# Layer 0's mixture of experts: rank products over all 128 rows, exponentials ahead of the codes' copy, sums and experts' products one whole tile later

## What is computed

```
q = einsum('btd,ed->bte', hidden_states, W_q)            # 4 heads, two halves x and y
sim = einsum('pbthn,hkpn->pbthk', q, keys)
scores_xy, idx_xy = top_k(sim, 8)
all_scores = sx[..., :, None] + sy[..., None, :]         # 64 pairs per head
scores, pk = top_k(all_scores, 8)
w = silu(einsum('btd,bthkd->bthk', hidden_states, down_embed[indices]) * softmax(scores))
experts_states = einsum('bthk,bthkd->btd', w, up_embed[indices])
dense = silu(hidden_states @ W_up.T) @ W_down.T
return dense + experts_states
```

## Time and profile before

| | us |
|---|---|
| median of 3 runs (1495.67 to 1496.87) | 1496.2 |
| the profiled execution's own time | 1500.19 |
| its span, first to last instruction | 1498.9 |
| feed-forward loop, first code to last expert product (208.39 to 509.86) | 301.5 |
| PE / DVE / ACT / POOL busy over the span | 1258.3 / 967.3 / 623.6 / 423.1 |

### The profile page before, as it was taken

The page is one execution under the profiler, slowest core; times in us unless marked ns, Lnnn a source line. Parts: engine busy times, 40 slices in busy tenths (PEclk is TensorE's granted clock), DMA queues, the critical chain, the costliest instruction groups (busy, mean ns, idle before and its releaser), DMA issues.

```text
span 1498.9 us, 23059 instructions
## 1 busy us (share of the span) xinstructions
PE 1258.3 (84%) x8094; PEld 828.3 (55%) x8094; DVE 967.3 (65%) x2897; ACT 623.6 (42%) x1625; POOL 423.1 (28%) x691
## 2 busy tenths in 40 slices
PE   5377669888988579999999999999999998577885
PEld 3266625555555446656666665566566665265555
DVE  3588777888876347766666566566666665365465
ACT  1000024444444235555555555555555554412331
POOL 1013241333313124343343333333433433101010
PEclk9598989999999769999999999999999999778797
DMA  6200020000000000000000000000000000000000
GB/s 181 78 1 1 1 85 1 1 1 1 1 1 1 0 0 1 1 2 1 1 1 2 1 1 1 1 1 1 1 1 1 1 1 1 0 3 5 8 8 8
DMA packets 18402, 15.33 MB, mean 10 GB/s; under 512 B 2416, under 2 KB 16752, under 8 KB 18160
## 3 DMA queue, kind: packets, MB, share of 16 engines
q1 hardware_dynamic: 18288, 13.86, 3.1%
HBM read 12.81 MB, written 1.05 MB: 9 GB/s over the span
## 4 chain that ended last, share of the span: by engine, by line
PE 62%; DVE 19%; ACT 9%; issue 7%; POOL 1%; SPq 0%; DMA 0%; DVEq 0%; ACTq 0%; POOLq 0%
PE bank L1395 11%; PE bank L1439 10%; PE bank L1405 8%; PE bank L1596 4%; ACT prb L1464 4%; PE bank L917 3%; PE bank L1349 3%; PE bank L1727 2%; PE bank L1380 2%; DVE negmax L1544 2%; DVE moe L1788 2%; PE bank L1372 2%; PE bank L1399 2%; PE bank L1359 2%; PE bank L902 2%
## 5 line engine op out<-in xcount | busy, mean ns | idle before, releaser
L1490 POOL TENSOR_SCALAR prb<-prb,rnorm 128x512 f32<-128x512 f32 (+3 forms) x512 | 272.5, 549 | 477.9 <-DVE rnorm L1561 475.7
L1464 ACT ACTIVATE prb<-bank,negmax 128x512 f32<-128x512 f32 (+3 forms) x512 | 264.4, 525 | 288.1 <-DVE negmax L1544 283.9
L1544 DVE TENSOR_REDUCE negmax<-bank 128x1 f32<-128x512 f32 (+3 forms) x512 | 219.2, 480 | 126.6 <-PE bank L1399 124.9
L1395 PE MATMUL bank<-kT,qT 64*128 64x512 f32 (+3 forms) x1024 | 202.2, 479 | 3.2 <-ACT prb L1464 3.2
L1405 PE MATMUL bank<-ident,prb 128*128 128x128 f32 x1280 | 193.0, 282 | 3.0 <-POOL prb L1490 1.9
L1405 PEld LDWEIGHTS bank<-ident,prb 128*128 128x128 f32 x1280 | 141.4, 142 | 49.5 <-issue 24.9
L1439 PE MATMUL bank<-prbT,vv 128*64 128x512 f32 (+3 forms) x1024 | 151.9, 439 | 1.7 <-issue 0.8
L1552 DVE COPY prbT<-bank 128x512 f32<-128x512 f32 x128 | 87.7, 685 | 87.0 <-PE bank L1405 87.0
L1395 PEld LDWEIGHTS bank<-kT,qT 64*128 64x128 f32 x1024 | 77.8, 186 | 52.7 <-issue 37.5
L1464 ACT ACTIVATION_READ_ACCUMULATOR prb<-bank,negmax 128x1 f32 x512 | 102.2, 200 | 0.0
L1439 PEld LDWEIGHTS bank<-prbT,vv 128*64 128x64 f32 x1024 | 63.8, 136 | 67.7 <-issue 60.4
(11 more groups left out here) (438 smaller groups left out, 2126.8 us busy)
## 6 DMA issues: line engine op xcount, KB each, us to landing
ew2T<-in_ew2T SPq DMA_DIRECT2D x1, 1024.0 KB, 6.4
ew<-in_ew SPq DMA_DIRECT2D x1, 1024.0 KB, 5.7
wq<-in_Wq SPq DMA_DIRECT2D x2, 512.0 KB, 4.9
wk<-in_Wk SPq DMA_DIRECT2D x2, 512.0 KB, 7.0
wv<-in_Wv SPq DMA_DIRECT2D x1, 1024.0 KB, 7.9
out<-res SPq DMA_DIRECT2D x16, 64.0 KB, 1.5
wmod<-in_wmod SPq DMA_DIRECT2D x2, 384.0 KB, 3.9
c_filt_sb<-in_c_filt SPq DMA_DIRECT2D x1, 768.0 KB, 7.0
```

The costliest lines, as they stand in the source:

```text
L1395: T.matmul(s_of(j, s, i, qc), q[r, qc * P:(qc + 1) * P], k[r, 0:(qc + 1) * P], start=True, stop=False)
L1464: A.activation(prb[j % 2][:, i, p_at[qc]:p_at[qc] + (qc + 1) * P], s_of(j, s, i, qc), ACT.Exp, bias=negmax[j % 2][:, place[qc], i:i + 1], ...
L1490: last = G.tensor_scalar(v, v, rnorm[j % 2][:, place[qc], i:i + 1], 1.0, ALU.mult, ALU.mult)
L1544: V.tensor_reduce(negmax[j % 2][:, place[qc], i:i + 1], s_of(j, s, i, qc), AX.X, ALU.max, negate=True).then_inc(at_max, 1)
```

## The change

1. `sel_y` and `sel_x` get rows of zeros, so that both rank products run over all 128 rows of `codeT`. The outputs are the same; the constants grow and `iota_y` and its neighbours move by 224 words.
2. ACT: `exp(n,0)` and `exp(n,1)` stand ahead of `keep_code(n)`, `keep_past_gate(n)` behind all four `exp`. `keep_sums` and PE's `sums`, `dense`, `experts` and DVE's `result` are done for tile n-2 in step n, one of each in every step.
3. PE: `logit(n,2)` stands between `code(n)` and the ranks, `logit(n,3)` behind ranks 0 and 1, `sums(n-2)` between these and ranks 2 and 3, and `dense(n-2)` and `experts(n-2)` behind them. Both `logit(n+1,.)` stand ahead of `down(n+1)`. Of the two `up` of an odd step the first stands ahead of them, the second behind `down(n+1)`, and from the second batch on both use bank 6.
4. ACT: at the end of an odd step all four `silu` of the two tiles stand in a row.

```diff
--- before.py
+++ after.py
@@ -244,13 +244,13 @@
         prob = [at.take(f"prob{i}", [P, PH, EXPERTS]) for i in range(3)]
         wT = at.take("wT", [P, EXPERTS // P, P])
         codeT = [at.take(f"codeT{i}", [P, 3 * P], BF16) for i in range(2)]
-        assert at.at <= 15264
-        at = Region(15264)
+        assert at.at <= 15040
+        at = Region(15040)
         iota_y = at.take("iota_y", [P, KEYS, TOP], BF16)
         iota_x = at.take("iota_x", [P, XROWS, TOP], BF16)
         rank_ident = at.take("rank_ident", [P, TOP, P], BF16)
-        sel_y = at.take("sel_y", [P, XROWS * KEYS], BF16)
-        sel_x = at.take("sel_x", [P, PH, EXPERTS], BF16)[0:PH * XROWS, :, :]
+        sel_y = at.take("sel_y", [P, 2, EXPERTS], BF16)
+        sel_x = at.take("sel_x", [P, PH, EXPERTS], BF16)
         assert at.at <= 2 * LANE
         at = Region(RAW + 6144)
         gT = [at.take(f"gT{i}", [P, I_UP // P, S]) for i in range(2)]
@@ -444,9 +444,8 @@
             for l in range(2):
                 A.activation(silT[:, l, :], cT[l][:, :], ACT.Silu).then_inc(silu_c, 1)
             for i in range(2):
-                r = slice(KEYS * i, KEYS * i + KEYS)
-                A.activation(sel_y[r, :].rearrange("q (i j) -> q i j", j=KEYS), ident[r, r].unsqueeze(1).broadcast_to([KEYS, XROWS, KEYS]),
-                             ACT.Copy).then_inc(const_ready, 1)
+                A.activation(sel_y[:, i, :].rearrange("q (i j) -> q i j", j=KEYS),
+                             ident[:, KEYS * i:KEYS * i + KEYS].unsqueeze(1).broadcast_to([P, XROWS, KEYS]), ACT.Copy).then_inc(const_ready, 1)
             A.wait_ge(lam_sum, 1)
             A.activation(lam_s[:, :], lam_s[:, :], ACT.Exp).then_inc(lam_exp, 1)
 
@@ -520,7 +519,7 @@
                 G.tensor_scalar(rank_ident[:, r, :], ident[:, :], 2.0 * TOP - 1 - r, 1.0, ALU.mult, ALU.mult)
             n = PH * XROWS
             G.tensor_copy(sel_x.rearrange("q h (i j) -> q (h i) j", j=KEYS),
-                          ident[0:n, 0:n].unsqueeze(2).broadcast_to([n, n, KEYS])).then_inc(const_ready, 1)
+                          ident[:, 0:n].unsqueeze(2).broadcast_to([P, n, KEYS])).then_inc(const_ready, 1)
 
 
 
@@ -833,6 +832,10 @@
 
             return [(n // NT + 1, n % NT - 1 + k) for k in range(2)] if n % 2 and n // NT + 1 < B else []
 
+        def up_bank(b, c):
+
+            return c % 2 if b == 0 else 0
+
         def normed_at(n):
 
             before = n // NT + 1 if n % NT == 0 and n // NT + 1 < B else None
@@ -855,10 +858,10 @@
                 free["sums"] = (w.h_ready, b + 1)
 
             def up(b, c):
-                where = ("sums", "out")[c % 2]
+                where = ("sums", "out")[up_bank(b, c)]
                 take(where)
                 T.wait_ge(pre.h_ready, b + 1)
-                T.matmul((SUMS, OUT)[c % 2][:, :], w_up[:, c * P:(c + 1) * P], hT[b % 2], start=True, stop=True).then_inc(ff_up, 1)
+                T.matmul((SUMS, OUT)[up_bank(b, c)][:, :], w_up[:, c * P:(c + 1) * P], hT[b % 2], start=True, stop=True).then_inc(ff_up, 1)
                 free[where] = (ff_silu, NT * b + c + 1)
 
             def tokens(n):
@@ -887,13 +890,13 @@
                 free["s"] = (ff_codeT, n + 1)
 
             def rank(n, h):
-                i, r = PH * n + h, slice(KEYS * (h % 2), KEYS * (h % 2) + KEYS)
+                i = PH * n + h
                 if h == 0:
                     T.wait_ge(ff_codeT, n + 1)
                 if i >= 2:
                     T.wait_ge(ff_mask, i - 1)
-                T.matmul(RANK[h % 2][:, :], codeT[n % 2][r, h // 2 * P:(h // 2 + 1) * P], sel_y[r, :], start=True, stop=False)
-                T.matmul(RANK[h % 2][:, :], codeT[n % 2][0:PH * XROWS, 2 * P:3 * P], sel_x[:, h, :], start=False, stop=True).then_inc(ff_rank, 1)
+                T.matmul(RANK[h % 2][:, :], codeT[n % 2][:, h // 2 * P:(h // 2 + 1) * P], sel_y[:, h % 2, :], start=True, stop=False)
+                T.matmul(RANK[h % 2][:, :], codeT[n % 2][:, 2 * P:3 * P], sel_x[:, h, :], start=False, stop=True).then_inc(ff_rank, 1)
 
             def logit(n, h):
                 i = PH * n + h
@@ -938,34 +941,36 @@
             for n in range(TILES):
                 before, after = normed_at(n)
                 code(n)
+                logit(n, 2)
                 rank(n, 0)
                 rank(n, 1)
+                logit(n, 3)
+                if n >= 2:
+                    sums(n - 2)
+                rank(n, 2)
+                rank(n, 3)
+                if n >= 2:
+                    dense(n - 2)
+                    experts(n - 2)
                 if n + 2 < TILES:
                     sim(n + 2)
-                for h in (2, 3):
-                    logit(n, h)
-                    rank(n, h)
-                if n % 2 == 0 and n:
-                    dense(n - 1)
-                    sums(n - 1)
-                    experts(n - 1)
                 if before is not None:
                     turned(pre, before)
                 if after is not None:
                     turned(post, after)
-                for b, c in up_at(n):
-                    up(b, c)
+                chunks = up_at(n)
+                if chunks:
+                    up(*chunks[0])
                 if n + 1 < TILES:
                     logit(n + 1, 0)
+                    logit(n + 1, 1)
                     down(n + 1)
-                    logit(n + 1, 1)
-                if n % 2:
-                    dense(n - 1)
-                    sums(n - 1)
-                    experts(n - 1)
-            dense(TILES - 1)
-            sums(TILES - 1)
-            experts(TILES - 1)
+                if chunks:
+                    up(*chunks[1])
+            for n in (TILES - 2, TILES - 1):
+                sums(n)
+                dense(n)
+                experts(n)
             turned(post, B - 1)
             yield
 
@@ -975,7 +980,7 @@
                 A.wait_ge(ff_up, NT * b + c + 1)
                 if b >= 2:
                     A.wait_ge(ff_out, NT * (b - 1))
-                A.activation(gT[b % 2][:, c, :], (SUMS, OUT)[c % 2][:, :], ACT.Silu).then_inc(ff_silu, 1)
+                A.activation(gT[b % 2][:, c, :], (SUMS, OUT)[up_bank(b, c)][:, :], ACT.Silu).then_inc(ff_silu, 1)
 
             def keep_sim(n):
                 A.wait_ge(ff_sim, n + 1)
@@ -1027,28 +1032,27 @@
             keep_sim(1)
             exps(0)
             for n in range(TILES):
-                keep_code(n)
-                keep_past_gate(n)
                 exp(n, 0)
                 exp(n, 1)
+                keep_code(n)
                 exp(n, 2)
                 exp(n, 3)
+                keep_past_gate(n)
+                if n >= 2:
+                    keep_sums(n - 2)
                 if n + 1 < TILES:
                     exps(n + 1)
                 if n + 2 < TILES:
                     keep_sim(n + 2)
-                if n % 2 == 0 and n:
-                    keep_sums(n - 1)
                 if n % 2:
                     for b, c in up_at(n):
                         silu_up(b, c)
                     silu_past(n - 1)
                     silu_past(n)
-                    silu(n - 1, 0)
-                    silu(n - 1, 1)
-                    silu(n, 0)
-                    keep_sums(n - 1)
-                    silu(n, 1)
+                    for m in (n - 1, n):
+                        silu(m, 0)
+                        silu(m, 1)
+            keep_sums(TILES - 2)
             keep_sums(TILES - 1)
             yield
 
@@ -1216,8 +1220,6 @@
                     statistics(post, after)
                 if more:
                     at = indices_of(n + 1)
-                if n % 2 == 0 and n:
-                    result(n - 2)
                 gate_of(n, 0)
                 if more:
                     cast = best_of(n + 1, *at)
@@ -1228,8 +1230,8 @@
                 gate_of(n, 3)
                 if more:
                     code_of(n + 1, cast)
-                if n % 2 == 0 and n:
-                    result(n - 1)
+                if n >= 2:
+                    result(n - 2)
                 if before is not None:
                     keep_before(before)
                 if after is not None:

```

## The result

| | before | changed |
|---|---|---|
| median of six runs each, us | 1496.9 (1495.7 to 1502.1) | 1507.3 (1505.1 to 1511.9) |
| ratio, with its 95% interval | | 1.0064 (1.0042 to 1.0085) |
| span of the profiled execution | 1498.9 | 1510.6 |
| feed-forward loop, first `code` to the end of the last `experts` | 301.5 | 313.9 |
| everything else of the span | 1197.4 | 1196.7 |

The change makes the kernel slower by 0.6%, and all of it lies in the one loop that it touches: +12.4 us there, -0.7 in the rest.

The account below looks back on a forecast made before the run. PE was taken as nearly the feed-forward loop's bound, DVE 3 us behind. Five pairs +15.1, step 0 +0.5, steps 13 and 14 -2.9, end -1.5 gave +11.2, scaled to 1507.5 us; range 1500 to 1513, chance 0.55.

Parts of the forecast that it names:

- The chain: Path round a pair of feed-forward steps through second up, ACT's block, exponentials and gates: 37.3 us, against 36.6 before.
- The odd step: Odd step of the five pairs: PE runs without a hole, 15.4 us instead of 18.3, gate 0 starting at 4.7.
- The payback: ACT's block behind the late second up puts prob(n+1,0) at 22.9; PE waits 6.4 us in logit(n+1,2).
- The clock: Each 6.4 us PE wait drops the clock to 1.2 GHz; slower products behind it cost 2.35 us a pair.
- Steps 0 to 2: Loop's start: step 0 takes 15.4 us against 14.91, steps 1 and 2 take 38.05 against 37.99.
- Steps 13 and 14: Late loop steps without up: 35.7 us against 38.59, with 1.3 for the clock after a 3.5 us wait.
- The end: Loop's end, where sums(14) waits for silu(14) until 12.6: 25.4 us against 26.84, including 1.5 for the clock.
- Ranks over 128 rows: Rank products with covered weight loads take 0.215 us each instead of 0.32; four cost 0.86 rather than 1.27.
- Rival (a): Clock holds or comes back at once behind PE's wait: pairs cost 37.3 us, total 1490.6; chance 0.10.
- Rival (b): ACT's block is off the path, exponentials come in time, each step takes 15.4 us: total 1451; chance 0.06.
- Rival (c): Rank weight loads stay bare: 1.3 us in each of 6 pairs, +8, total 1515; chance 0.19 shared with another rival.

Follow-up runs that it names:

- e6: Changed kernel plus six idle float32 products on PE between code and the waiting logit in even steps 2 to 12; 1497.4 us, ratio 0.9996.
- e7: Kernel before with only the rank products changed, to run over all 128 rows; 1483.3 us, ratio 0.9893.
- e4: Changed kernel with both up earlier on PE, and silu_past and silu of tile n-1 right behind the first silu_up on ACT; 1469.9 us.
- e9: Changed kernel with PE's first up early, second between logits and down; ACT does tile n-1's silu_past and silu first, second silu_up last; 1470.7 us.
- e5: Changed kernel with only the rank products put back to 64 and 32 rows; 1528.4 us, ratio 1.0194.
- e1: Changed kernel with the past gate's copy again ahead of exp(n,2) and exp(n,3); 1504.0 us, ratio 1.0033.
- e2: Changed kernel with only ACT's order changed: in odd steps silu_past and both silu of tile n-1 stand between the two silu_up; 1498.4 us.
- e10: e9 with the past gate's copy again ahead of exp(n,2); 1466.4 us, ratio 0.9776.

## Why the forecast held, and where it was off

The forecast was 1507.5 us, slower, and the median is 1507.3. The chain held to about 1 us; that the medians meet within 0.2 is luck, since the loop came 1.2 above the forecast and the rest of the span 0.7 below, and the profiled execution lay 4.6 above its median where 4.0 was taken. Step by step:

- **The odd step**, 15.4: measured 15.33. Its second `up` ends at 314.59 + 0.86, 15.3 behind `code` (15.4); gate 0 starts at 4.72 (4.7).
- **The payback**: `prob(n+1,0)` stands at 322.32 + 0.69, 22.9 behind `code` (22.9). The wait is 6.41 (6.4), gate 0 to the next `code` 10.65 (10.7).
- **The clock**, 2.35 a pair: low from 320.0 to 326.8, back 3.7 us after the work resumed; e6 puts the mean at 2.28. It is not the same in every pair: in the one from 3 the clock came back only 6 us after the work had resumed, within the 3.4 to 6.6 that the forecast took from the earlier trace rows. A pair 39.53 (39.65), five of them +14.5 (+15.1).
- **Steps 0 to 2**: 15.36 and 38.10 (15.4 and 38.05).
- **Steps 13 and 14**, 35.7: measured 37.04. The chain up to the wait's end was right, 20.1 (20.0). The term that was mis-sized is the clock's, which I had put at half (1.3) because the wait is short. It is 3.46 us, and yet the products behind it ran at the lower level throughout, which costs the whole 2.6.
- **The end**, 25.4: measured 25.8. The `sums` that wait start at 12.8 (12.6). The loop is +12.4 where +11.2 was forecast, most of the difference from steps 13 and 14; the rest of the span is 0.7 less, where the forecast had 0.
- **Ranks over 128 rows**: 0.22 a product, as taken. The rule of the Trainium skill that a load overlaps only with another row group ("TensorE: Matmul & The Clock Gate", "Part 3: Packing small matmuls — row/col tiling") is contradicted for full rows by e7's starts at 0.22.
- **Rival (a)**, the clock holds: e6 makes this case, and its pairs are the 37.3 named there.
- **Rival (b)**, ACT's block off the path, needed the second `up` by about 9. e4 and e9 come near it another way, by taking `silu` out from behind it: pairs of 32.8, where (b) had two steps of 15.4, that is 30.8, and DVE's own work takes 30 us a pair.
- **Rival (c)** was priced at 1.3 a pair and 8 us; e5 shows 2.8 and 21. The rival's price failed because it counted the eight loads of the odd step and half as many of the even one, and not the products behind the groups nor the longer slow clock. That the first part alone is worth 15 us in the kernel before (e7) was therefore missed too; the forecast did not need it, since the change has both. Of the change's four parts, then, the first gives about 15 us and the new order with all its moves takes about 24 (1507.3 against 1483.3, from two chips whose kernel before differs by 2 us). The two do not simply add: in the new order the first part is worth 20 (e5), and without it the new order takes 30 (1528.4 against 1498.7).

## What to carry to other kernels

An engine's queue is a chain of its own: before moving a step behind a late producer, list what stands behind its consumer on the other engine, and let work whose data is ready go first. Two moves of a few lines (e4) turned a change of +0.6% into -1.9%, with the same instructions. The largest wait in the list is named after the one that came last; follow what that one was queued behind (e1 against e2). And add to the price of an idle stretch of PE the slower products behind it: here they cost 2.3 us behind a wait of 6.4, and filling the wait with useless products took that price away.

## What the runs showed of the hardware that I had not expected

- PE's rank products over 64 and 32 rows in turn cost 0.32 us each and those over 128 rows 0.22, for the same 512 columns, and the full-row product behind a short-row group pays 0.1 as well. It is not the row count alone: in the attention of the kernel before, two float32 products of 512 columns over 64 rows, one in each half of the array's rows, take 0.96 together (below), where one over 128 rows takes 0.86. Whether in the ranks the changing row count or the overlapping rows cost the 0.1, no run separates.

```profile
810.16 1.13 PE L1395 MATMUL bank<-kT,qT 64*128 64x512 f32 x4
811.12 0.28 PE L1399 MATMUL bank<-masks 64*128 64x128 bf16 x4
```

- In the six pairs that wait 6.4 us (5.3 in the first of the changed kernel's) the granted clock was low for 10 to 14 us where short-row products followed (e5), and for 7 us in five and 10 in one where full-row products did (changed).
- The length of a wait did not settle whether the clock fell. It was low behind waits of only 1.8 us (e9, e10) in some pairs and not in others with the same wait: in e9 three of five kept 1.00. In e4 it stayed at 1.00 behind two waits of 3.0 us, and in the changed kernel it fell behind one of 3.46.
